# Four written steps in each turn of the loop over blocks, with two more entries in the table of step words

## What is computed

```python
def _L0_ffn_ref(x, gate_w, w1, w3, w2):
    logits = jnp.einsum('btd,de->bte', x, gate_w)
    probs = jax.nn.softmax(logits, axis=-1)
    expert_weights, expert_indices = jax.lax.top_k(probs, TOP_K)      # TOP_K = 2
    expert_weights = expert_weights / expert_weights.sum(-1, keepdims=True)
    out = jnp.zeros_like(x)
    for i in range(E):                                                # E = 8
        wi = jnp.where(expert_indices == i, expert_weights, 0.0).sum(-1)
        h = jax.nn.silu(jnp.einsum('btd,df->btf', x, w1[i])) * jnp.einsum('btd,df->btf', x, w3[i])
        out = out + jnp.einsum('btf,fd->btd', h, w2[i]) * wi[..., None]
    return out
...
x = x + _L0_xattn_ref(_layernorm(x, axis=-1), ctx_2048, mask_BxS2_if0, ...)
x = x + _L0_ffn_ref(_layernorm(x, axis=-1), ...)
```

## Time and profile before

| | |
|---|---|
| median of three runs | 444.62 us (444.39 to 445.95) |
| the profiled execution | 445.63 us |
| its span, first to last instruction | 443.8 us |
| granted TensorE clock, mean | 0.97 |
| busy: TensorE matmuls / weight loads | 405.7 us (91%) / 338.6 us (76%) |
| busy: VectorE / GpSimd / ScalarE | 303.2 us (68%) / 243.2 us (55%) / 193.7 us (44%) |
| TensorE in the chain that ended last | 70% of the span |
| bytes moved | 89.82 MB, 202 GB/s |

### The profile page before, as it was taken

One profiled execution on the slowest core, in us unless ns is written; L12 is line 12 of the kernel. 1 busy time (PEld: TensorE's weight loads), 2 busy tenths in 40 slices (PEclk: granted clock), 3 DMA queues, 4 the chain that ended last, 5 costly groups with the idle time before them and its releaser, 6 DMA issues.

```text
span 443.8 us, 12041 instructions
## 1 busy us (share of the span) xinstructions
PE 405.7 (91%) x2300; PEld 338.6 (76%) x2305; DVE 303.2 (68%) x826; ACT 193.7 (44%) x335; POOL 243.2 (55%) x251
## 2 busy tenths in 40 slices
PE   0669899969899999999999999999999999999983
PEld 0557686536678888888888888888888888788873
DVE  7995959887775577647775775577587546857450
ACT  2573527104543454335544553455445335634341
POOL 6328444313664676546665685576577445435443
PEclk9997969698999999999999999999999999999998
DMA  6953996702895788567887787789788655465652
GB/s 188 356 172 100 303 358 206 289 26 58 265 278 177 198 259 246 178 168 194 243 264 209 228 250 205 194 247 251 202 265 254 197 159 152 127 154 130 166 144 36
DMA packets 80362, 89.82 MB, mean 202 GB/s; under 512 B 8071, under 2 KB 60583, under 8 KB 80343
## 3 DMA queue, kind: packets, MB, share of 16 engines
q1 hardware_dynamic: 64327, 55.24, 38.4%
q0 software_dynamic: 16016, 34.37, 30.7%
HBM read 58.77 MB, written 30.82 MB: 202 GB/s over the span
## 4 chain that ended last, share of the span: by engine, by line
PE 70%; issue 3%; DVE 3%; ACT 1%; DMA 1%; DVEq 1%; POOL 0%; ACTq 0%; POOLq 0%
PE bank L1545 67%; PE bank L1552 2%; ACT split L341 1%; DMA out<-yblk,itok 1%; PE bank L1488 1%; DVE onehot_lo L1173 0%; POOL out L546 0%; ACT yblk L718 0%; DVE hT L1288 0%; DVE hmul L1272 0%; DVEq L295 0%; DVE swap_in L1280 0%; ACTq L341 0%; PE bank L1481 0%; DVE ctx_sb L951 0%
## 5 line engine op out<-in xcount | busy, mean ns | idle before, releaser
L1545 PE MATMUL bank<-split,xT_hi 128*128 x592 | 166.1, 402 | 4.4 <-issue 2.7
L1545 PEld LDWEIGHTS bank<-split,xT_hi 128*128 128x128 f32 x592 | 106.5, 189 | 27.9 <-issue 8.6
L1545 PEld LDWEIGHTS bank<-split,hT 128*128 128x128 f32 x888 | 111.5, 189 | 5.5 <-issue 1.5
L1545 PE MATMUL bank<-split,hT 128*128 (+1 forms) x888 | 113.3, 284 | 1.4 <-ACT yblk L718 0.7
L711 ACT ACTIVATE gact<-bank 128x512 f32<-128x512 f32 x74 | 44.3, 598 | 138.5 <-PE bank L1545 136.2
L1272 DVE TENSOR_TENSOR hmul<-gact,bank 128x512 f32<-128x512 f32 x74 | 50.8, 686 | 74.4 <-ACT gact L711 73.8
L1545 PE MATMUL bank<-split,xT_lo 128*128 x296 | 92.2, 393 | 0.0
L529 POOL DMA_INDIRECT xblk<-z_rows,gidx x40 | 41.0, 1024 | 89.6 <-DVE gidx L1295 69.8
L546 POOL DMA_INDIRECT out<-yblk,itok x37 | 71.0, 1919 | 32.1 <-issue 29.6
L347 DVE TENSOR_TENSOR split<-raw,split x22 | 50.3, 2292 | 25.9 <-ACT split L341 24.2
L1545 PEld LDWEIGHTS bank<-split,xT_lo 128*128 128x128 f32 x296 | 55.6, 188 | 12.3
(11 more groups left out here) (199 smaller groups left out, 336.0 us busy)
## 6 DMA issues: line engine op xcount, KB each, us to landing
raw<-in_L_ffn_w POOLq DMA_DIRECT2D x84, 256.0 KB
swap_rows<-swap_in SPq DMA_DIRECT2D x74, 256.0 KB, 3.7
swap_out<-swap_rows SPq DMA_DIRECT2D x74, 256.0 KB, 3.7
ctx_sb<-in_ctx SPq DMA_DIRECT2D x4, 1024.0 KB, 6.4
raw<-in_L_ffn_w SPq DMA_DIRECT2D x12, 256.0 KB, 6.6
x_all<-in_x SPq DMA_DIRECT2D x4, 512.0 KB, 8.4
depool_rows<-gact SPq DMA_DIRECT2D x4, 512.0 KB, 4.0
out<-x_all SPq DMA_DIRECT2D x4, 512.0 KB, 6.2
```

Source lines behind the costliest of these rows:

```text
L1545: mm = pe.matmul(out_, xp, w_, start=start and n == 0, stop=stop and n == 2)
```

## The change

The loop's turn holds four written steps in place of two, each inside the test of the step before it. The trip count is the number of fours that cover the blocks after the first two (10). The table has two more entries (45).

```diff
-STEP_PAIRS = BLOCKS // 2
-TABLE = 2 + 2 * STEP_PAIRS + 3
+STEP_FOURS = -(-(BLOCKS - 2) // 4)
+TABLE = 2 + 4 * STEP_FOURS + 3
...
-            with eng.Fori(0, STEP_PAIRS) as pair:
-                word = step_word(eng, pair * 2 + 2)
+            with eng.Fori(0, STEP_FOURS) as four:
+                word = step_word(eng, four * 4 + 2)
                 with eng.If(word & F_RUN):
-                    body(pair * 2 + 2, 0, pair + 1, word)
-                    word = step_word(eng, pair * 2 + 3)
+                    body(four * 4 + 2, 0, four * 2 + 1, word)
+                    word = step_word(eng, four * 4 + 3)
                     with eng.If(word & F_RUN):
-                        body(pair * 2 + 3, 1, pair + 1, word)
+                        body(four * 4 + 3, 1, four * 2 + 1, word)
+                        word = step_word(eng, four * 4 + 4)
+                        with eng.If(word & F_RUN):
+                            body(four * 4 + 4, 0, four * 2 + 2, word)
+                            word = step_word(eng, four * 4 + 5)
+                            with eng.If(word & F_RUN):
+                                body(four * 4 + 5, 1, four * 2 + 2, word)
```

## The result

The changed kernel took 452.17 us (median of four runs, 450.67 to 454.59), the kernel before 444.50 us in the runs beside it. The ratio is 1.018, with an interval of 1.012 to 1.025. The forecast was 442.6 us with a range of 441.0 to 446.0, so the change went the other way by 7.7 us. The profiled execution took 451.47 us, 449.9 of it span.

A forecast was written before the change was run, and what follows sets the result against it. TensorE or its sequencer was taken to bound the loop. Borders gain 2.1 us, the table costs 0.1, the rest nothing: 2.0 us off the 444.62 us median gives 442.6 us, range 441.0 to 446.0.

The forecast's parts named there:

- The bound and the border's price: In the loop TensorE is the bound; a border between turns costs its sequencer 0.22 us more than one inside.
- Step (5): Doubled loop code on every engine: GpSimd reload likely, 1.4 to 3.7 us a transfer, priced at nothing; TensorE none.
- step (1): TensorE's turns: nine borders move inside a turn and gain 2.1 us, between 2.0 and 2.6.
- Rival C's second place: GpSimd's loop: three transfers of 3.7 us a turn pass its 7.4 us, costing 30 us; chance 0.13 for both places.
- Its first place: TensorE's four-step code doesn't stay, each jump back waits for a transfer: 454 to 473 us; chance 0.13 for both places.
- Rival B: Another engine falls late where new weights are split and takes up the border's gain: 443.5 to 444.9 us; chance 0.20.
- Step (2): The same borders on the other four engines: shorter borders there only mean more waiting, so the end gains nothing.
- Step (3): Inner words, nested tests and index expressions of each step: nothing taken, 1.3 us if there were no lead.
- Step (4): Two more table columns, once ahead of the loop and on the path: 0.1 us for all.

The follow-up runs named there:

- the control: The kernel before, two steps in a turn, with GpSimd's fetch of the weight column moved to the beginning of its step: 442.50 us against 443.00, ratio 0.998.
- the kernel with the early fetch: The changed kernel with GpSimd's fetch of the weight column moved to the beginning of its step: 444.36 us, ratio 1.003.

## Why the prediction was wrong, point by point

*The bound and the border's price* were right. TensorE bounds the loop; a border between turns costs 0.2 us of its sequencer; nine of them went and gave 2.8 us in this trace against 2.1. The border into step 8, to which I gave 0.3 us, gave 0.82. The load of the step word was not slow there in the changed run (305 ns), but that is not all: with loads of 433 and 510 ns the stretch takes 8.58 and 8.62 us in the kernels with four on TensorE alone and on all but GpSimd, and 9.12 us with 556 ns in the control with two. In the kernel with four on GpSimd alone it takes 9.03 us with a load of only 309 ns. So in these traces this border is long with the jump and short without it, whatever the load, and 0.3 us was too little. In the stretches these two kernels bear the sum out: the nine that moved take 77.9 and 77.7 us together, and 79.7 to 80.9 in the kernel before, the control and the kernel with 20 instructions added. Their whole traces, 1.9 and 1.8 us shorter than that of the kernel before, and their medians, 0.8 and 1.0 us, with intervals of 0.4% to each side, can't tell 1 us from 2.

*Step (5) failed*, in the price at the end and not in what happens. I wrote that a reload on GpSimd was likely, and it came, though not for my reason: GpSimd's is not the longest body, its loop has 234 instructions in the compiled program before and TensorE's 297. I bounded it by 1.4 to 3.7 us for one transfer; it was about 4.5 us a turn, since GpSimd waits twice, behind the jump and soon after it. I then set it against 7.4 us of GpSimd's own waiting in a turn and took nothing. There were two errors in that.

First, the waiting of a late engine isn't its margin. The margin belongs to whoever reads what it makes. I named the gather, the column and the add as queued behind the stall and said they are read a step later; that holds for the gather and the add, as the kernel with the early fetch shows. The column is read by ScalarE a step later, too, but VectorE waits for its landing before it overwrites the index that the fetch reads, in the middle of its step. That wait was in the trace of before, with 2.2 us, and a wait that already shows has a margin of nothing in some steps. The 5.9 us from 161.80 to 167.67 were there to be read as well.

Second, the waiting isn't where the lateness falls. A turn's 7.4 us lie in steps without weight pieces; in steps with pieces GpSimd works through the earlier trace rows, so what one jump adds stays for several steps. I said that the next steps would give it back; they did so after the reader had waited. Of 8 x 4.5 = 36 us some 9 came through to the loop's time, the 6.6 us lost and the 2.8 that the borders gave; the rest was covered, and my price took all of it to be.

The empty last turn was counted (17 + 1 + 1 turns, step (1)) and then left out of (5): its jump stands on the path to the end, 3.0 us whatever the loop does. The wait that showed, the upper bound of 3.7 us a transfer and the empty turn's jump were all in the trace of before, and by them the sign was open at least; the 4.5 us a turn were not.

*Rival C's second place* was the right engine with the wrong threshold: "past its 7.4 us at three transfers". It decided at about 4.5 us a turn, well below that; where between nothing and 4.5 the loss begins, no run shows. With 0.13 on both places of C together its chance was too low, and so was the upper end of the range. *Its first place*, TensorE, was wrong for four steps and right for sixteen.

The Trainium skill, "Runtime: NRT & Kernel Launch", section "Instruction fetch mechanics", said what came: a taken branch to code outside what is held forces a fetch. That TensorE holds more than GpSimd agrees with the runs: its loop of four steps stays with 590 instructions (7 packets in the whole run), GpSimd's doesn't with 462. The size doesn't agree: the page's 32 KiB are 512 instructions there, and GpSimd's loop with 60 added, 297 instructions in the compiled program, doesn't stay, nor does that of four steps with 462; with 257 it stays. The measurement decides. Whether length alone sets the edge, or also where the loop begins in memory, no run tests. I used the sizes to place the miss and then priced the place at nothing; counted out, 462 fit into 512, so that the place was right is luck. *Rival B* is half right by its form (another engine takes up what the border gave), and its 444.9 was too low by the same missing wait.

*Step (2)* was right: four steps on TensorE alone are within 0.2 us of four on all but GpSimd. *Step (3)* was right as far as a trace shows: stretches inside a turn where nothing is late (into 5, into 17) take 8.61 us in both kernels. *Step (4)*, the table, was not tested by itself; in the changed trace the two comparisons take 902 ns each in place of 868, as the sum had it.

## What to carry to other kernels

Before a loop body is doubled, look at each engine's code by itself: here it was neither the busiest engine nor the one with the longest body whose loop no longer stayed. Then every jump back costs microseconds, the one into an empty last turn too. To price a delay on a side engine, take for each thing it makes the time from its landing to the first instruction that waits for it, waits before an overwrite included; the engine's own idle time alone doesn't give it. Where only one engine profits from longer turns, lengthen that one alone, and if its code is too long for a loop, write it out straight: here that took 439.12 us, and a loop that had to be read again 454.03.

## What the runs showed of the hardware that was not expected

The edge is sharp: a GpSimd loop with 20 instructions added runs with 13 packets in the whole run, with 60 it reads 100 and takes 49 us more. Code that is never run counts like code that is. On TensorE the reload lies inside the branch instruction (5158 and 3690 ns against 209 as a rule for the jump back of four steps), on GpSimd in the gap behind it. It costs TensorE clock as well: behind the idle 4.91 us the granted clock was 0.50 for 4 us, the lower of its two levels (1.2 GHz). And straight code is free on TensorE here: 35 steps read once, in 26 packets of 16 KB, left no gap in its products.
